# A four-layer graph network: a tile's gathered chunks are turned in four pieces between other steps, and the wait for a split load is rebuilt

## The chip, the cores and the metric

The kernel runs on one core of one Trainium2 chip. The metric is the device time of one execution, in microseconds (us). Engines are named as in the profile: PE (matmuls; PEld is its weight load), DVE (vector), ACT (scalar), POOL (GpSimd) and SP (which issues DMAs). One execution was also taken by the hardware profiler; all rows are of that execution.

## What is computed

Four graph layers run one behind the other on 3125 nodes of 128 features and 103125 edges sorted by destination, each as `x = x + layer(relu(layernorm(x)))`: a graph convolution, an attention with additive scores (4 heads), a second attention (GAT, 2 heads), and an interaction layer with a filter for each edge. The one that the change touches most is the additive attention:

```python
projected = (x @ W).reshape(N, HEADS, OUT_CH)          # 4 heads of 32
src = projected[row]
dst = projected[col]
scores = jnp.tanh(src + dst)
scores = jnp.einsum('ehc,hc->eh', scores, att)
scores = jnp.exp(scores - jnp.max(scores, axis=0, keepdims=True))
out = jax.ops.segment_sum(src * scores[:, :, None], col, num_segments=N)
normalizer = jax.ops.segment_sum(scores, col, num_segments=N)
out = out / jnp.maximum(normalizer, 1e-12)[:, :, None]
```

## The kernel before

The sorted edges are cut into 202 tiles of 512; a tile is four chunks of 128 edges, and its destinations lie in a window of 20 nodes. A stage (`Stage`) is one program for each engine, and semaphores alone order the engines against each other. `over_tiles` (L77) writes each engine's loop: it is given pairs of a lag and a piece of work, and in step s it calls each piece, in the order of the list, for tile s less its lag. So the list is the order of the engine's instructions, and a wait in one piece holds up all that is behind it. The steps of the first `head` rings are written out, the rest is a hardware loop.

`attend` (L1973) is that stage for both attention layers. The additive layer is the case `gat=False`: one bank of z per tile (`a.zs` is 1), 12 slots for gathered rows (`ring`), 6 for windows (`held`). In it

- SP loads, for two tiles at a time, the destinations and the window's rows (L1457, L1462); it waits for `z_ready` of a tile six earlier.
- POOL gathers the 512 source rows of a tile by four indirect DMAs of a chunk each (L897). Before a tile it waits for `sums_ready` of the tile that had its slot, 12 earlier.
- PE has four pieces. `scores` (lag 3) is one matmul with `far` (L2101) and one with `att` (L2109) and gives `score_ready`. `features` (lag 1) turns the four chunks by f32 transposes into the z bank (L2088), each once its chunk has landed, adds the window's rows by one matmul (L2092), and gives `z_ready`; ahead of that it waits for the window, for the one-hots, and for `act_ready` of the tile two earlier, which had the same z bank. `turn` (lag 4) transposes the raised scores (L2119, and in some steps the merge of running maxima, L1764 to L1777) and gives `turned`. `sums` (lag 5) is eight f32 matmul passes over the gathered rows (L2144) and gives `sums_ready`.
- ACT takes `exp` of the scores (L2178, lag 3), `tanh` of z (L2172, lag 1; it gives `act_ready`), and copies the sums (L2190, lag 5).
- DVE makes the one-hots (L1477, lag 0), finds the top score (L2228, L2230, lag 3), and copies the turned weights (L2246, lag 4), which gives `weight_ready`.

PE's order is set by the list in the last lines of its program: scores, features, turn, sums. In the GAT layer (`gat=True`) features has two heads, so eight transposes and two window matmuls, and its list is another.

`sum_counted` (L1348) is the second convolution's stage. It multiplies stored count matrices, in groups of 24 tiles (3000 KB a load), with node features. Before it, one tile's counts (`k.rebuild` is 1) are made again: DVE makes the one-hots, PE counts, ACT evicts, SP stores them (L1378) and waits for the store. The first group's 3000 KB are loaded in three thirds (L1375) ahead of that, each with a semaphore `begun[i]`; PE waits for `loaded[0]`, which SP gives after the store (L1387), and ahead of each third for `begun[i]` to reach a value held in a register, `k.rebuild * 16 + 16`. The next group's load is issued at L1390.

## Time and profile before

| what | value |
|---|---|
| time, median of 3 runs | 4942.16 us |
| lowest and highest run | 4939.04, 4942.38 us |
| the profiled execution's span | 4898.1 us, 89702 instructions |
| mean granted TensorE clock over the span | 0.852 |
| PE busy | 3999.0 us (82%) |
| POOL busy | 2828.1 us (58%) |
| DVE busy | 2847.4 us (58%) |
| ACT busy | 1737.4 us (35%) |

In the profile's rows "L2088" is line 2088 of the code, the arrow names the program's buffers, out<-in, and the brackets at a row's end hold the time for which the engine stood idle before it and what ended that. "issue" there is idle time in which the engine waited for nothing that the profile shows, and "remote" is an event that the profile puts down to no instruction. The additive loop fills 679 to 1922 us of the span and the GAT loop about 2100 to 3350.

### The profile page before, as it was taken

To read this page: it belongs to the slowest core of one execution; us is meant where nothing else is said; L and a number is where in the kernel's file an instruction comes from. 1 tells how busy PE (TensorE), PEld (TensorE's weight loads), DVE (VectorE), ACT (ScalarE), POOL (GpSimd) and SP (SyncE) were. 2 spreads that over 40 slices of the span, in tenths; PEclk is the share of its full clock that TensorE was granted. 3 is DMA by queue.
4 is the path that set the end of the run, shared out by engine and by line. 5 is a ranking of instruction groups with operands and counts; after the bars stand their busy time and mean duration, and the time that the engine had idled before them with its cause. 6 is when DMAs were issued, how large, how long until landed. Compare 5 with 4: busy or idle time off the path is not lost. (4 is left out here: it accounts for less than half of the span.)

```text
span 4898.1 us, 89702 instructions
## 1 busy us (share of the span) xinstructions
PE 3999.0 (82%) x22566; PEld 2260.3 (46%) x22566; DVE 2847.4 (58%) x8457; ACT 1737.4 (35%) x4474; POOL 2828.1 (58%) x3060
## 2 busy tenths in 40 slices
PE   3997927788887877488888888885399999999987
PEld 1344414445544544344444444442256655556652
DVE  7994032333333334555555555556678888888868
ACT  3773023344344334333333333331322222222227
POOL 0122356666666663555555555554368888888862
PEclk8998957776777777688988888886699999999999
DMA  2333422222222221333333333330056666666650
GB/s 80 91 87 103 147 71 57 57 56 57 57 56 57 56 57 27 113 98 96 97 97 96 96 97 96 97 96 18 21 97 104 105 105 104 104 105 104 104 110 13
DMA packets 377425, 402.41 MB, mean 82 GB/s; under 512 B 86457, under 2 KB 322502, under 8 KB 377030
## 3 DMA queue, kind: packets, MB, share of 16 engines
q0 software_dynamic: 151904, 198.72, 21.0%
q1 hardware_dynamic: 225382, 202.21, 14.4%
q8 instruction: 43, 0.70, 0.1%
q14 instruction: 96, 0.79, 0.1%
HBM read 312.91 MB, written 87.78 MB: 82 GB/s over the span
## 5 line engine op out<-in xcount | busy, mean ns | idle before, releaser
L897 POOL DMA_INDIRECT gathered<-table,sources x952 | 903.6, 949 | 600.6 <-issue 259.9
L1709 POOL DMA_INDIRECT sums<-gathered,idx x606 | 988.7, 1632 | 217.8 <-issue 166.4
L1571 PE MATMUL bank<-wide 128*128 128x512 bf16 x3636 | 851.5, 379 | 0.0
L2228 DVE TENSOR_REDUCE neg_raw<-bank 80x1 f32<-80x512 f32 (+1 forms) x404 | 276.6, 685 | 725.9 <-remote 252.1
L897 POOL DMA_INDIRECT wide<-table,sources x464 | 438.7, 946 | 275.1 <-issue 125.7
L1571 PEld LDWEIGHTS bank<-wide 128*128 128x128 bf16 x3636 | 347.7, 98 | 364.1 <-issue 1.7
L2178 ACT ACTIVATE msg<-bank,neg_top 80x512 f32<-80x512 f32 (+1 forms) x404 | 275.7, 682 | 643.1 <-DVE neg_top L2230 353.6
L1222 POOL TENSOR_TENSOR acc<-acc,msg 128x20 f32 x404 | 108.3, 268 | 411.2 <-issue 244.6
L2221 DVE TENSOR_TENSOR zact<-zact,bank 128x512 f32<-128x512 f32 x404 | 259.5, 683 | 123.1 <-ACT zact L2170 72.9
L2106 PE MATMUL bank<-zact,att_cells 128*32 128x512 f32 x808 | 289.4, 732 | 37.9 <-issue 36.2
L2088 PEld LDWEIGHTS bank<-ident,gathered 128*128 128x128 f32 x1360 | 191.8, 165 | 258.0 <-issue 232.2
L2109 PE MATMUL bank<-zact,att_cells 128*80 128x512 f32 x404 | 301.6, 838 | 6.6 <-issue 6.6
L2246 DVE COPY edge_rows<-bank 128x320 f32<-128x320 f32 (+1 forms) x404 | 183.2, 453 | 203.5 <-remote 132.7
L2144 PE MATMUL bank<-edge_rows,gathered 128*128 128x80 f32 x1088 | 193.9, 337 | 92.5 <-DVE edge_rows L2246 81.9
L2088 PE MATMUL bank<-ident,gathered 128*128 128x128 f32 x1360 | 237.4, 317 | 35.4 <-issue 26.4
L2119 PE MATMUL bank<-ident,msg 80*128 80x80 f32 (+1 forms) x1616 | 215.5, 262 | 61.5 <-issue 33.9
L897 POOL DMA_INDIRECT h_nm<-table,sources x200 | 189.4, 947 | 130.5 <-DMA wide<-table,sources 69.3
L2190 ACT COPY partial<-bank 32x20 f32 (+1 forms) x808 | 132.6, 164 | 357.5 <-remote 239.5
L1169 DVE TENSOR_SCALAR gathered<-iota_c,partial 128x500 f16<-128x500 f16 x808 | 257.6, 339 | 1.7 <-issue 1.3
L2170 ACT ACTIVATE zact<-bank 128x512 f32<-128x512 f32 x404 | 216.8, 588 | 98.1 <-DMA window<-parts 81.2
L1178 PE MATMUL bank<-gathered,zact 128*128 128x500 f16 x812 | 209.3, 381 | 49.4 <-ACT zact L1285 28.1
L1622 ACT COPY gathered<-bank 128x437 f32<-128x437 f32 x202 | 106.1, 525 | 337.0 <-PE bank L1597 249.7
(406 smaller groups left out, 7603.9 us busy)
## 6 DMA issues: line engine op xcount, KB each, us to landing
zact<-in_src_flat SPq DMA_DIRECT2D x202, 192.0 KB
edge_rows<-in_attr_rows SPq DMA_DIRECT2D x202, 128.0 KB
dst_pair<-local_rows SPq DMA_DIRECT2D x177, 128.0 KB
gathered<-table,sources POOLq DMA_INDIRECT x952
dst_pair<-local_rows SPq DMA_DIRECT2D x202, 64.0 KB
counts<-wide SPq DMA_DIRECT2D x4, 3000.0 KB
counts<-fm_ab SPq DMA_DIRECT2D x4, 3000.0 KB
fm_ab<-counts SPq DMA_DIRECT2D x4, 3000.0 KB, 11.0
```

The costliest lines, as they stand in the source:

```text
L897: pool.indirect_dma_start(out=g[:, j, :], out_offset=None, in_=table, in_offset=bass.IndirectOffsetOnAxis(ap=mine, axis=0)).then_inc(rows_ ...
L1169: hot = dve.tensor_scalar(k.cell_hot[slot][:, j, :], k.iota_c[:, :], own, None, ALU.is_equal)
L1571: pe.matmul(k.bank[b][:, :], k.split[t.two][:, c, :], k.source_hot[t.two][:, b * CHUNK:(b + 1) * CHUNK], start=first, stop=c == PARTS - 1, ...
L1709: pool.indirect_dma_start(out=k.sums[j], out_offset=bass.IndirectOffsetOnAxis(ap=k.idx[t.slot][:, j:j + 1], axis=0), in_=out_rows(t)[:, j, ...
L2088: pe.matmul(z_bank(t, h)[:, j * P:(j + 1) * P], g[:, j, h * F:(h + 1) * F], k.ident[:, :], is_transpose=True, start=(j == 0), stop=False, ...
L2106: mm = pe.matmul(score_bank(t)[own_cells(h), :], a.att[h][:, own_cells(h)], k.zact[t.two][:, h, :], start=False, stop=True, skip_group_che ...
L2109: mm = pe.matmul(score_bank(t), a.att[0][:, :], k.zact[t.two][:, 0, :], start=False, stop=True)
L2119: mm = pe.transpose(weight_bank(t)[:, j * cells:(j + 1) * cells], raised(t)[:, j * P:(j + 1) * P], k.ident[lanes(t), lanes(t)])
L2170: act.mul(k.zact[t.two][:, h, :], z_bank(t, h)[:, :], 0.2).then_inc(slope_ready, 1)
L2178: act.activation(raised(t), score_bank(t), ACT.Exp, bias=k.neg_top[lanes(t), bass.ds(t.t, 1)], accum_out=k.weight_sum[lanes(t), bass.ds(t. ...
L2221: m = dve.tensor_tensor(za, za, z_bank(t, h)[:, :], ALU.max)
L2228: dve.tensor_reduce(raw, score_bank(t), AX.X, ALU.max, negate=True).then_inc(top_found, 1)
```

## The change

In `attend`, `features` is cut into four functions: `features_begin` (the waits for the one-hots and the z bank, a semaphore increment, chunk 0), `features_second`, `features_third`, and `features_end` (the wait for the window, chunk 3, the window matmul, `z_ready`). In the additive layer PE's list becomes: first piece, scores, second piece, turn, third piece, sums, last piece. The GAT layer keeps one `features`, which calls the four in a row.

In `sum_counted` SP loads two thirds ahead of the store instead of three; after the store it waits for the second of them, tells PE by `second_there`, and loads the last third. PE waits for constants (or for the loop's counter) where it waited for a register's value.

```diff
--- before.py
+++ after.py
@@ -1354,6 +1354,7 @@
             hot_ready, counted, evicted, stored, free = (st.sem("hot_ready"), st.sem("counted"), st.sem("evicted"),
                                                          st.sem("stored"), st.sem("free"))
             loaded, begun = [st.sem(f"loaded{i}") for i in range(2)], [st.sem(f"begun{i}") for i in range(3)]
+            second_there, rounds_done = st.sem("second_there"), st.sem("rounds_done")
             summed, kept, adds_begun, added = st.sem("summed"), st.sem("kept"), st.sem("adds_begun"), st.sem("added")
             thirds = [(i * GROUP // 3, (i + 1) * GROUP // 3) for i in range(3)]
 
@@ -1367,18 +1368,26 @@
                 @block.sync
                 def _(sp):
                     sp.sem_inc(free, 1)
-                    for landed in begun:
+                    for landed in begun[0:2]:
                         sp.sem_inc(landed, 16)
+
+                    def load_third(i):
+                        lo, hi = thirds[i]
+                        sp.dma_start(k.counts[0][:, lo:hi, :], k.all_counts[lo:hi, :, :].rearrange(
+                            "t p c -> p t c")).then_inc(begun[i], 16)
                     with sp.Fori(0, k.rebuild) as n:
-                        for (lo, hi), landed in zip(thirds, begun):
-                            sp.wait_ge(landed, n * 16 + 16)
-                            sp.dma_start(k.counts[0][:, lo:hi, :], k.all_counts[lo:hi, :, :].rearrange(
-                                "t p c -> p t c")).then_inc(landed, 16)
+                        for i in range(2):
+                            sp.wait_ge(begun[i], n * 16 + 16)
+                            load_third(i)
                         sp.wait_ge(evicted, n + 1)
                         sp.dma_start(k.all_counts[bass.ds(tile(n), 1), :, :].rearrange("t p c -> (t p) c"),
                                      again).then_inc(stored, 16)
                         sp.wait_ge(stored, n * 16 + 16)
                         sp.sem_inc(free, 1)
+                        sp.wait_ge(begun[1], n * 16 + 32)
+                        sp.sem_inc(rounds_done, 1)
+                    sp.sem_inc(second_there, 1)
+                    load_third(2)
 
                     def load(now):
                         if now is None:
@@ -1409,6 +1418,7 @@
                     with pe.Fori(0, k.rebuild) as n:
                         pe.wait_ge(hot_ready, n + 1)
                         cell_counts(k, pe, 0, k.bank[0]).then_inc(counted, 1)
+                        pe.wait_ge(begun[0], n * 16 + 32)
 
                     def sums(now):
                         if now is None:
@@ -1416,8 +1426,10 @@
                         pe.wait_ge(loaded[now.par], (now.pair + 1) * 16)
                         wait_count(pe, kept, now.g - 1)
                         for i, (lo, hi) in enumerate(thirds if first(now) else [(0, now.size)]):
-                            if first(now):
-                                pe.wait_ge(begun[i], k.rebuild * 16 + 16)
+                            if first(now) and i == 1:
+                                pe.wait_ge(second_there, 1)
+                            if first(now) and i == 2:
+                                pe.wait_ge(begun[2], 16)
                             for b in range(k.blocks):
                                 mm = block_sums(k, pe, parts, now, b, lo, hi)
                         mm.then_inc(summed, 1)
@@ -2076,23 +2088,41 @@
             def _(pe):
                 turn_locals(k, pe, lo)
 
-                def features(t):
-
-                    pe.wait_ge(win_loaded[t.slot % held], (held_rounds(t) + 1) * 16)
+                def turn_rows(t, j):
+                    g = rows(t)
+                    pe.wait_ge(rows_loaded[t.slot][j], (t.rounds + 1) * 16)
+                    for h in range(a.zs):
+                        pe.matmul(z_bank(t, h)[:, j * P:(j + 1) * P], g[:, j, h * F:(h + 1) * F],
+                                  k.ident[:, :], is_transpose=True, start=(j == 0), stop=False,
+                                  skip_group_check=True)
+
+                def features_begin(t):
                     pe.wait_ge(onehot_t_ready, t.t + 1)
                     wait_count(pe, act_ready, t.t - 1)
-                    g = rows(t)
-                    for j in range(SUB):
-                        pe.wait_ge(rows_loaded[t.slot][j], (t.rounds + 1) * 16)
-                        for h in range(a.zs):
-                            pe.matmul(z_bank(t, h)[:, j * P:(j + 1) * P], g[:, j, h * F:(h + 1) * F],
-                                      k.ident[:, :], is_transpose=True, start=(j == 0), stop=False,
-                                      skip_group_check=True)
+                    pe.sem_inc(turns_begun, 1)
+                    turn_rows(t, 0)
+
+                def features_second(t):
+                    turn_rows(t, 1)
+
+                def features_third(t):
+                    turn_rows(t, 2)
+
+                def features_end(t):
+                    pe.wait_ge(win_loaded[t.slot % held], (held_rounds(t) + 1) * 16)
+                    turn_rows(t, 3)
                     for h in range(a.zs):
                         mm = pe.matmul(z_bank(t, h)[:, :], window(t)[0:WROWS, h * F:(h + 1) * F],
                                        place_hot(t)[0:WROWS, :], start=False, stop=True,
                                        skip_group_check=True)
                     mm.then_inc(z_ready, 1)
+
+                def features(t):
+
+                    features_begin(t)
+                    features_second(t)
+                    features_third(t)
+                    features_end(t)
 
                 def scores(t):
 
@@ -2155,7 +2185,8 @@
                     over_tiles(pe, k.tiles, [(3, scores), (1, features), (6, turn_sums), (4, turn_top), (4, turn),
                                              (5, sums)], ring=ring)
                 else:
-                    over_tiles(pe, k.tiles, [(3, scores), (1, features), (4, turn), (5, sums)], head=3, ring=ring)
+                    over_tiles(pe, k.tiles, [(1, features_begin), (3, scores), (1, features_second), (4, turn),
+                                             (1, features_third), (5, sums), (1, features_end)], head=3, ring=ring)
                     merge.tail_turns(pe)
 
             @block.scalar
```

## Rows read from the trace of the kernel before

**Rows 1.** The head of the page

```profile
span 4898.1 us, 89702 instructions
```

**Rows 2.** Windows view: stretch: its length, busy us by engine (count), PEclk, DMA

```profile
core 0: us, PE busy (x) PEld busy (x) DVE busy (x) ACT busy (x) POOL busy (x), PEclk, DMA share, GB/s
...
760.00:1890.00 1130.00, 922.40 (x3952) 559.86 (x3952) 374.47 (x1216) 456.90 (x1412) 704.04 (x744) 0.73 0.22 57
1893.00:1918.00 25.00, 23.68 (x146) 15.50 (x146) 14.66 (x52) 18.22 (x60) 0.00 (x0) 1.00 0.03 2
2120.00:3330.00 1210.00, 1024.93 (x7136) 537.89 (x7137) 684.53 (x1880) 383.77 (x939) 711.81 (x752) 0.88 0.33 96
```

**Rows 3.** Timeline, PE, end of the additive loop: start us, duration us

```profile
1896.12 0.41 PE L2101 MATMUL bank<-onehot_t,far 64*80 64x512 bf16 x1
...
1897.38 0.60 PE L2088 MATMUL bank<-ident,gathered 128*128 128x128 f32 x4
...
1898.23 0.50 PE L2119 MATMUL bank<-ident,msg 80*128 80x80 f32 x4
...
1899.55 0.41 PE L2101 MATMUL bank<-onehot_t,far 64*80 64x512 bf16 x1
```

**Rows 4.** Timeline, PE, one step at 1.2 GHz, same columns

```profile
1176.29 0.65 PE L2101 MATMUL bank<-onehot_t,far 64*80 64x512 bf16 x1
...
1182.62 0.65 PE L2101 MATMUL bank<-onehot_t,far 64*80 64x512 bf16 x1
```

**Rows 5.** Line L897 in 760:1890: what ended its engine's idle time, us, times

```profile
  issue: 208.5, 650
  remote: 163.5, 62
  PE bank L2144: 54.2, 32
```

**Rows 6.** Timeline, all engines, around 1115

```profile
1115.03 0.60 PE L2092 MATMUL bank<-onehot_t,window 60*128 60x512 bf16 x1
1115.42 0.94 POOL L897 DMA_INDIRECT gathered<-table,sources  x1 [0.30 <-issue]
...
1115.57 0.80 PE L2119 MATMUL bank<-ident,msg 80*128 80x80 f32 x4
1118.63 0.60 ACT L2172 ACTIVATE zact<-bank 128x512 f32<-128x512 f32 x1 [5.14 <-remote]
...
1118.92 0.47 DVE L2246 COPY edge_rows<-bank 128x320 f32<-128x320 f32 x1
...
1119.55 1.18 POOL L897 DMA_INDIRECT gathered<-table,sources  x1 [3.19 <-remote]
```

**Rows 7.** Timelines of DVE and POOL, opening stretch of the loop

```profile
732.82 0.49 DVE L2246 COPY edge_rows<-bank 128x320 f32<-128x320 f32 x1 [25.19 <-remote]
...
738.02 0.94 POOL L897 DMA_INDIRECT gathered<-table,sources  x1 [8.79 <-remote]
```

**Rows 8.** Waits view, PE, 760:1890: us, times, longest

```profile
PE bank L2144 <- DVE edge_rows L2246: 71.9, 25, 7.1
...
PE bank L2088 <- issue: 1.4, 3, 0.7
```

**Rows 9.** Sum_counted: timelines of SP and PE, then DMA issues (us to landing)

```profile
459.32 0.37 SPq L1378 DMA_DIRECT2D counts<-fm_ab  x1
...
465.17 0.45 PE L1195 MATMUL bank<-wide,h_nm 128*128 128x160 f16 x2 [6.74 <-SPq L1387]
...
482.63 0.57 PE L1195 MATMUL bank<-fm_ab,h_nm 128*128 128x480 f16 x2
...
wide<-counts SPq DMA_DIRECT2D x3, 1000.0 KB, 7.7
fm_ab<-counts SPq DMA_DIRECT2D x1, 3000.0 KB, 12.3
counts<-fm_ab SPq DMA_DIRECT2D x1, 125.0 KB, 5.5
```

## The prediction, made before the changed kernel ran

> **What bounds the kernel now.** I read the page's head first (span 4898.1 us, one core) [rows 1], then the windows view, stage by stage [rows 2]. The change touches three loops. In the additive loop (760 to 1890) 744 gathers, so 186 tiles of four, take 1130 us: 6.08 us a tile. PE is busy 922.40 us of it, at a mean granted clock of 0.73. Two rows at a granted clock of 1.00, one step apart, give PE's work for one tile alone: 1899.55 - 1896.12 = 3.43 us [rows 3]. At the lower level (1.2 GHz) the same step takes 1182.62 - 1176.29 = 6.33 us [rows 4]. So PE at the upper level would need far less than 6.08 and at the lower level more: the loop flips between the two, and PE's share says little.
>
> Next the gathers, by line: the groups of POOL's idle time before L897 [rows 5]. They add up to 208.5 + 163.5 + 54.2 = 426.2 us. A gather followed at once by the next shows 0.30 us, 744 x 0.30 = 223; the other 203 us are true waits, in 62 + 32 = 94 stretches: one per 1.98 tiles, 2.16 us long. Without them a tile costs POOL 4 x (0.94 + 0.30) = 4.97 us, the floor.
>
> What are these waits? The timeline around 1115 shows it [rows 6]. PE's window matmul is over at 1115.6, yet ACT's tanh, which needs it, starts at 1118.63 after idling 5.14 us; DVE's copy starts at 1118.92 though the turns it reads (L2119, seen at 1115.57) were over by 1116.4; POOL had begun its last gather at 1115.42. Three engines start within 0.3 us, and POOL 0.6 us later. In the opening stretch POOL streams 12 tiles of gathers: DVE idles 25.19 us before a copy, and POOL itself 8.79 us [rows 7]. So while gathers stream, what PE finishes reaches the others late, in bursts, and most reach them when POOL stops. I take as the bound: POOL's floor, plus a stop each time that PE has run dry of answers.
>
> The Trainium skill (page "SBUF — State Buffer", section "Who interferes with whom") says that DMA has its own ports and contends with no engine. By it these late starts would have some other cause than the gathers' traffic; the rows only show that they go together.
>
> **Additive loop: what is removed, added, moved.** The four turns of a tile's chunks (L2088) no longer stand together behind the scores, but one ahead of the scores, one behind them, one behind the turn, one behind the sums, and there the window matmul and z_ready. One sem_inc is added per tile. The engine work is the same: no matmul more or fewer. Were chunks late, pieces would help; PE's waits hold only 1.4 us (3 times) before L2088 in 186 tiles, against 71.9 us before L2144 [rows 8]. So the waits on chunks are worth nothing: 0 (bounds: -1.4 to +6, the latter 186 x 0.03 us for a sem_inc, a sixth of what POOL's smallest gap holds for waits and bookkeeping, an estimate).
>
> What changes is when z_ready comes: from behind the scores to the end of the step, 1899.55 - 1898.23 = 1.3 us later [rows 3], while its user stands where it stood or earlier: the first piece of tile t waits for the tanh of tile t-2 (same bank) and now heads the step, ahead of scores, turn and sums, which are queued behind it. Before, two whole steps lay between a tile's z and that wait; now one.
>
> The price by counting: a step gives four results, and I ask, from the moment when nothing more is passed on, how many PE can finish, the first withheld one included, until a wait needs an answer to a withheld one. A tile's turn comes one step behind its scores, its sums one step behind its turn.
> Order before (scores, features, turn, sums): scores first withheld: next step's turn stops PE, 6 done; features first: the turn after it is withheld too, next step's sums stop PE, 6; turn first: 5; sums first: 7. Mean 6.0.
> Order after (scores, turn, sums, features): scores first: 5; turn first: 5; sums first: 6 (stopped by the first piece two steps on); features first: 5, stopped by the same. Mean 5.25.
> A stretch now holds 1.98 tiles, eight results: six ahead and two that are passed on in between. With the same two, 7.25 instead of 8. Then 94 stretches become 94 x 8 / 7.25 = 103.7, each with 2.16 us: +21.0 us in 186 tiles, x 202 / 186 = **+22.8 us**. Bounds: 0, if bursts come by time and not by how far PE gets; +52, if PE's pace at 1.2 GHz becomes the pace (rival B). I take 22.8 because the wait that was longest before, L2144 on DVE's copy [rows 8], is of just this kind: turn to sums, a result and its answer.
>
> SP's window loads wait for z_ready of a tile six earlier, so they also go 1.3 us later, with some five steps in hand, 17 us at 3.43 and more at 6.08: 0. ACT and DVE keep their orders; the tanh is asked for beside the copy of the sums. 0.
>
> **GAT loop** (2120 to 3330) [rows 2]: the four pieces run back to back as before; the window wait stands behind three chunks instead of ahead, and a sem_inc per tile is added. POOL is busy 711.81 of 1210 us there, PE 1024.93, the clock 0.88. A window that is waited for later can only help, a sem_inc at 0.03 us costs 202 x 0.03 = 6 at most: 0, bounds -5 to +6.
>
> **sum_counted.** Three thirds of 1000 KB are in flight together (landing 7.7 us, median); the store of a tile's counts is issued at 459.32, lands after 5.5 us, and PE starts at 465.17 after 6.74 us [rows 9]. With two thirds ahead of it, the store has 1 MB less before it. The three thirds were 3.0 MB in 10.0 us by their median pace (7.7 us is the second of three, 3.85 us a third, less as the queue fills): the store gains at most one third, 3.5 us, less 0.4 for the issue of the last third that now stands ahead of the next load on SP, and the new wait on the second third lies before the store's landing. Taken: -2.6. The last third, then issued near 462.5, is needed at two thirds of the first group: PE needs 482.63 - 465.17 = 17.5 us for all, so 11.6 us later, and a third alone landed in under 7.7. The next group's load takes 12.3 us with 17.5 us of cover, 5.2 to spare; the last third ahead of it costs up to 3.5 of these. If that cover were gone, the rest would show as a wait ahead of the second group, +1. So **-2.6**, bounds -3.5 to +1.
>
> **Sum.** The profiled execution took 4898.1 us, the median of the runs 4942.2, so 44.1 us lie around the span and stay. 4898.1 + 22.8 - 2.6 = 4918.3; with 44.1: **4962.4**. Own range of this case: 4942 + 0 - 3 to 4942 + 45: 4940 to 4987.
>
> **Rivals.**
> A, the order doesn't matter. The bursts go by POOL's stops and not by how far PE gets; the four pieces give PE the same work in other order, and nothing waited for chunks [rows 8]. Left are -2.6 and the sem_incs: 4936 to 4946, 4940. For it: POOL resumes on the sums of a tile 12 back, far behind. Against it: the 71.9 us on one answer.
> B, slower still. The first piece, now at the head of a step, holds up all that is queued behind it until the tanh comes; PE stands idle more, its clock stays at 1.2 GHz, and PE's own step, 6.33 us [rows 4], takes the place of 6.08. 202 x (6.33 - 6.08) = +50.5, so 4990. It decides from where the tanh of a tile comes over one step behind its z; the idle 5.14 us before ACT's tanh [rows 6] is already longer than the 3.43 us step.
> C, faster. Between results PE now always has a piece of a turn to do: a stop for one answer is covered by pieces, its idle time (1130 - 922 = 208 us) is broken up, and the clock holds the upper level longer; or sums close earlier in a step, so that POOL's stretches run longer. Whole, POOL's floor: 202 x (6.08 - 4.97) = -224, 4718; a third of it: -75, so 4942 - 75 - 3 = 4864. For it: 2 of the 3 worst waits are for DVE and ACT, not for data. Against it: a piece takes 0.15 us (0.60 for four [rows 3]) and the waits are some 3 us long.
> The Trainium skill (page "TensorE: Matmul & The Clock Gate", section "HAM oscillation — how this bites in real kernels") says that idle gaps between bursts of matmuls send the clock to half and that keeping PE fed restores it. By that the pieces would bring case C; by the row (0.15 us) each is too short to fill a 3 us gap. The trace agrees so far that the clock is 0.73 here and 1.00 at the loop's end, where no gather runs [rows 2].
>
> **Chances.** Forecast 0.34, A 0.21, B 0.13, C 0.32. C is large because the loop stands 224 us over its floor and any change of phase between PE, ACT and POOL may win a part, where at most some 50 can be lost by B. Slower by over 0.2% (9.9 us, about what a measurement of this kernel can tell from no change): 0.34 + 0.13 = 0.47; within: 0.21; faster: 0.32. Range for 8 in 10: 4880 to 5015, which leaves out the larger part of C beyond its -62 (0.13) and what lies beyond B (0.06); the likeliest case's own range is 4940 to 4987.
>
> **What would show it.** Right: in the windows view the additive loop goes from 6.08 to some 6.19 us a tile, POOL busy the same; POOL's waits before L897 count over 100 instead of 94, of the same 2.2 us; PE has a new wait ahead of the first piece, on ACT's tanh, of some 10 us or more; L2144's wait is no larger. In sum_counted PE starts near 462.5 with no gap ahead of the last third. GAT within 5 us. B: clock near 0.5 and the first piece as PE's largest wait. C: clock over 0.8, or under 80 waits of POOL. A: the same counts with the work in other order. It would be wrong altogether if POOL's waits change in length and not in number, since the count alone carries my sum.

## The result

The changed kernel takes 4951.13 us, median of 19 runs, against 4942.38 us of 19 runs of the kernel before, timed beside it: a ratio of 1.0017, 95% interval 1.0011 to 1.0023, so 8.8 us slower. The direction is the forecast one. The size is not: the forecast was +20.2 us, and the measured loss lies below the 0.2% that the prediction drew as its own line.

The profile after, first the windows view of the two attention loops, columns as in [rows 2]:

```profile
760.00:1890.00 1130.00, 958.57 (x3868) 562.80 (x3868) 368.47 (x1194) 445.66 (x1382) 695.41 (x732) 0.69 0.21 56
2120.00:3330.00 1210.00, 1011.07 (x7015) 531.36 (x7015) 671.59 (x1846) 377.47 (x925) 699.01 (x739) 0.87 0.33 95
```

732 gathers, 183 tiles, in 1130 us are 6.17 us a tile (6.08 in [rows 2]; 6.19 was forecast). That near match is luck: `z_early_3`, below, whose order should have kept the old pace, has 732 gathers in the same window too. PE is busier, 958.57 for 922.40 us, at a mean granted clock of 0.69 for 0.73. What ended POOL's idle time before its gathers (us, times), to be set beside [rows 5]:

```profile
  issue: 197.7, 630
  remote: 186.3, 76
  PE bank L2174: 51.2, 26
```

76 + 26 = 102 stops of POOL, one per 1.79 tiles, where 103.7 in 186 tiles were forecast, also one per 1.79. (By this count `z_early_3` has 100.) They last (197.7 + 186.3 + 51.2 - 732 x 0.30) / 102 = 2.11 us. PE's waits in the same stretch (us, times, longest), the pieces of features at L2095, the sums at L2174:

```profile
PE bank L2095 <- issue: 49.1, 22, 6.1
PE bank L2174 <- DVE edge_rows L2277: 47.8, 21, 5.6
...
PE bank L2095 <- ACT zact L2203: 12.2, 4, 5.0
```

The new wait ahead of the first piece is there, 49.1 + 12.2 = 61.3 us; the long ones all stand behind the window matmul (L2115) that closes the step before. The wait for DVE's copy is down from 71.9 [rows 8] to 47.8.

In `sum_counted` the timelines of SP and PE and the DMA issues (us to landing) answer to [rows 9]:

```profile
459.78 0.37 SPq L1383 DMA_DIRECT2D counts<-fm_ab  x1
462.42 0.37 SPq L1376 DMA_DIRECT2D wide<-counts  x1
...
462.89 0.45 PE L1195 MATMUL bank<-wide,h_nm 128*128 128x160 f16 x2 [3.99 <-SPq L1396]
...
481.11 0.57 PE L1195 MATMUL bank<-fm_ab,h_nm 128*128 128x480 f16 x2
...
fm_ab<-counts SPq DMA_DIRECT2D x1, 3000.0 KB, 14.8
counts<-fm_ab SPq DMA_DIRECT2D x1, 125.0 KB, 2.2
```

The store lands after 2.2 us for 5.5, PE starts at 462.89 for 465.17, the last third costs no wait, and the second group follows at 481.11 for 482.63 without a gap.

These two profiles should not be subtracted, though. The span after is 4945.2 us, 47 more than before's 4898.1, when the medians differ by 8.8. The profiled execution of after took 4946.96 us, 1.8 more than its span. So what lies around a span is some 2 us, and the 44.1 us that the prediction put there were something else: the profiled execution of before was faster as a whole than its timed runs, of which the fastest took 4935.64 us. It looks like an execution on another chip. From its first gather to its last the GAT loop takes 1305.5 us there, and 1302.7 to 1310.3 us in the four traces of the chip on which before takes 4906 us (below); after's takes 1326.5 us, and the traces of two chips on which before takes 4942 and 4934 us have 1323.2 to 1330.8 us, all with the GAT loop as before. The additive loop differs in the same way, 1217.1 to 1222.6 us against 1235.4 to 1254.2, whatever its order. So the steps from [rows 2] and [rows 5] to the rows above show the chip more than the change.

### The profile page after: what moved, and what is told of

It reads as the page before. It is cut to its first block and busy times, and to the rows that moved or that the text cites. A ratio compares the mean times of both kernels' runs of the same rounds, so it can differ in the third digit from the quotient of the medians.

```text
span 4945.2 us, 89965 instructions
## 1 busy us (share of the span) xinstructions
PE 4063.0 (82%) x22463; PEld 2281.6 (46%) x22566; DVE 2847.9 (58%) x8457; ACT 1737.1 (35%) x4474; POOL 2830.2 (57%) x3060
## 5 line engine op out<-in xcount | busy, mean ns | idle before, releaser
L897 POOL DMA_INDIRECT gathered<-table,sources x952 | 904.2, 950 | 633.2 <-issue 258.8
L1583 PE MATMUL bank<-wide 128*128 128x512 bf16 x3533 | 829.2, 379 | 5.6 <-issue 0.2
L897 POOL DMA_INDIRECT wide<-table,sources x464 | 439.9, 948 | 277.4 <-issue 128.5
L2095 PE MATMUL bank<-ident,gathered 128*128 128x128 f32 x1360 | 331.3, 334 | 70.8 <-issue 48.6
L2095 PEld LDWEIGHTS bank<-ident,gathered 128*128 128x128 f32 x1360 | 213.1, 176 | 294.7 <-issue 293.7
L2139 PE MATMUL bank<-zact,att_cells 128*80 128x512 f32 x404 | 321.3, 889 | 0.0
L2203 ACT ACTIVATE zact<-bank 128x512 f32<-128x512 f32 x202 | 119.6, 592 | 478.6 <-remote 340.1
L897 POOL DMA_INDIRECT h_nm<-table,sources x200 | 189.3, 946 | 135.4 <-DMA wide<-table,sources 62.9
L2201 ACT ACTIVATE zact<-bank 128x512 f32<-128x512 f32 x404 | 216.8, 588 | 94.0 <-DMA window<-parts 76.8
L2149 PEld LDWEIGHTS bank<-ident,msg 80*128 80x128 f32 (+1 forms) x1616 | 174.3, 167 | 145.5 <-issue 132.8
L2174 PE MATMUL bank<-edge_rows,gathered 128*128 128x80 f32 x1088 | 182.3, 325 | 54.6 <-DVE edge_rows L2277 39.4
```

What stands on the lines that cost most here:

```text
L897: pool.indirect_dma_start(out=g[:, j, :], out_offset=None, in_=table, in_offset=bass.IndirectOffsetOnAxis(ap=mine, axis=0)).then_inc(rows_ ...
L1583: pe.matmul(k.bank[b][:, :], k.split[t.two][:, c, :], k.source_hot[t.two][:, b * CHUNK:(b + 1) * CHUNK], start=first, stop=c == PARTS - 1, ...
L2095: pe.matmul(z_bank(t, h)[:, j * P:(j + 1) * P], g[:, j, h * F:(h + 1) * F], k.ident[:, :], is_transpose=True, start=(j == 0), stop=False, ...
L2139: mm = pe.matmul(score_bank(t), a.att[0][:, :], k.zact[t.two][:, 0, :], start=False, stop=True)
L2149: mm = pe.transpose(weight_bank(t)[:, j * cells:(j + 1) * cells], raised(t)[:, j * P:(j + 1) * P], k.ident[lanes(t), lanes(t)])
L2201: act.mul(k.zact[t.two][:, h, :], z_bank(t, h)[:, :], 0.2).then_inc(slope_ready, 1)
```

## The experiments

The change's form of `sum_counted` (the mend) is in all of them, with its waits on constants, so `mend_alone` is the base. Each was timed beside the kernel before on the same chip: 11 runs (`far_twice` 6, `one_gather` 2 each time) against 17 to 33 of before. A "stop" is a stretch in which POOL waits between two gathers.

**The parts one at a time.** `mend_alone`: the change's `sum_counted`, both attention layers as before.

> Only sum_counted is changed (two thirds ahead of the store, constant waits); both attention layers are as before. Theory (look-ahead count): -2 to -3 us, PE starts the first group near 462.9 as in the changed kernel, and the additive loop runs at 6.08 us a tile with a stop of POOL per 1.98 tiles. Rival (the profiled execution of before, 4898.1, is not typical of its 4942): the additive and the GAT loop are longer here than in that profile, by up to 40 us together, and the time is still -2 to -3 us against before.

Measured: 4903.31 us, before 4906.45; ratio 1.0000 (0.9991 to 1.0009). The medians give -3.1 us, the means of the same runs +0.2, and the interval doesn't exclude 0. The chip was another: before takes 4906 us on it and 4942 on the first.

`order_alone`, on top of it the additive order; the GAT layer's `features` untouched:

```diff
-over_tiles(pe, k.tiles, [(3, scores), (1, features), (4, turn), (5, sums)], head=3, ring=ring)
+over_tiles(pe, k.tiles, [(1, features_begin), (3, scores), (1, features_second), (4, turn),
+                         (1, features_third), (5, sums), (1, features_end)], head=3, ring=ring)
```

> mend_alone plus the additive layer's order in four pieces; the GAT layer's features are untouched. Theory (look-ahead count): +20 us against mend_alone, POOL stops once per 1.79 tiles instead of 1.98. Rival (the order costs half of that, and before's profile was a lucky one): +8 to +13 us against mend_alone, and all that the changed kernel lost.

Measured: 4913.41 us, 1.0018 (1.0009 to 1.0027), +10.1 us against `mend_alone` by the medians and +7.9 by the means: the rival's size. The windows view and POOL's idle groups, `mend_alone` first, then `order_alone`:

```profile
760.00:1890.00 1130.00, 898.19 (x3912) 542.68 (x3912) 372.74 (x1210) 454.24 (x1401) 704.40 (x744) 0.74 0.22 57
...
  issue: 205.6, 658
  remote: 167.4, 61
  PE bank L2156: 52.9, 25
```

```profile
760.00:1890.00 1130.00, 952.22 (x3929) 560.45 (x3930) 374.57 (x1208) 454.57 (x1407) 709.16 (x744) 0.70 0.22 57
...
  issue: 203.4, 647
  remote: 155.3, 64
  PE bank L2185: 63.4, 33
```

The stops go from 61 + 25 = 86 to 64 + 33 = 97, 13% more, where 10% were forecast. But their sum goes from 425.9 - 223.2 = 202.7 to 422.1 - 223.2 = 198.9 us: each is shorter, 2.05 for 2.36 us. PE is busy 952.22 for 898.19 us at a clock of 0.70 for 0.74. PE's waits tell the same as in after's profile, here on one chip, `mend_alone` first:

```profile
PE bank L2156 <- DVE edge_rows L2258: 99.0, 32, 8.3
```

```profile
PE bank L2095 <- issue: 51.8, 30, 5.2
PE bank L2185 <- DVE edge_rows L2288: 45.1, 20, 5.1
...
PE bank L2095 <- ACT zact L2214: 15.7, 8, 5.1
```

But neither trace shows where the 8 to 10 us are. Both windows hold 744 gathers, and from the first to the last gather the loop takes 1222.2 us in `mend_alone` and 1222.5 in `order_alone`. The profiled execution of `mend_alone` was the slowest of its 11 runs (4913.48 us), that of `order_alone` the second fastest (4910.60 us), so one pair of traces can't resolve a difference of that size.

How the lengths of stops differ shows when POOL's timeline is sorted by how many tiles it gathered since its last stop (gaps of over 0.6 us between two gathers, without the first and last tiles; the length less the 0.30 us of every gap):

| kernel | 1 tile: stops, us | 2 tiles | 3 tiles |
|---|---|---|---|
| before | 10, 1.67 | 50, 2.10 | 20, 2.93 |
| after | 17, 1.67 | 61, 2.26 | 12, 3.04 |
| mend_alone | 3, 2.16 | 52, 2.17 | 23, 2.94 |
| order_alone | 19, 1.58 | 55, 2.02 | 14, 2.83 |

A stop behind one tile takes about 1.6 us (in the rows with ten or more), behind two 2.1, behind three 2.9. A line through these gives an estimate: some 0.65 us for each tile that is let through and 0.95 us for the stop itself. If the lengths come about in this way, only the second part is paid more often when the same tiles come in more stops. This was drawn up after the result, and the sums of the two traces don't confirm it: by it 11 more stops would add some 10 us, where the sum of `order_alone` is no larger.

`gat_alone`: the GAT layer's `features` in four calls in a row with the added increment, the additive layer as before.

> mend_alone plus the GAT layer's features in the new form (one more semaphore increment per tile, the window's wait behind three chunks); the additive layer is as before. Theory: within 3 us of mend_alone. Rival (the added increment is the GAT loop's +22 us of the two profiles): +10 to +22 us against mend_alone.

Measured: 4908.39 us, 1.0003 (0.9994 to 1.0012), +5.1 against `mend_alone` by medians (+1.1 by means) with intervals that overlap. The GAT stretch, `mend_alone` first, then `gat_alone`:

```profile
2120.00:3330.00 1210.00, 1027.50 (x7118) 538.62 (x7119) 684.17 (x1877) 382.96 (x938) 708.25 (x749) 0.87 0.34 96
```

```profile
2120.00:3330.00 1210.00, 1020.50 (x7137) 535.08 (x7136) 684.36 (x1873) 383.47 (x937) 711.60 (x750) 0.88 0.34 96
```

749 and 750 gathers in the same 1210 us: the same pace. The rival's 10 to 22 us fall; a loss up to 5 us stays possible. By medians the parts are -3.1, +10.1 and +5.1, together +12.1; by means they are +0.2, +7.9 and +1.1, together +9.2. The whole was measured at +8.8 by both.

**Place or pieces.** `whole_last`: features whole, at the step's end.

```diff
-over_tiles(pe, k.tiles, [(3, scores), (1, features), (4, turn), (5, sums)], head=3, ring=ring)
+over_tiles(pe, k.tiles, [(3, scores), (4, turn), (5, sums), (1, features)], head=3, ring=ring)
```

> mend_alone plus the additive order scores, turn, sums, features, with features whole: the window's result stands at the same place as in the change, with no pieces. Theory (look-ahead count; the place of a tile's result counts, not the pieces): as order_alone within 5 us. Rival (the pieces matter, as cover for a wait or by the first piece heading the step): more than 8 us from order_alone, on either side.

Measured: 4908.59 us, 1.0004 (0.9995 to 1.0013): +5.3 against `mend_alone`, 4.8 below `order_alone`, and 80 stops of over 0.6 us where `mend_alone` has 77 and `order_alone` 91. By the letter the time is within the 5 us of the theory, but the stops are not: the count of results ahead gives 5.25 here as for `order_alone`. Features waits for a tanh at the end of a step now, but the scores at its head wait for the same tanh, and there PE does wait in this trace (L2150, the matmul with `att`):

```profile
PE bank L2150 <- issue: 65.6, 12, 7.9
...
PE bank L2150 <- ACT zact L2213: 18.7, 8, 8.6
```

So two orders with one count have 80 and 91 stops. PE's clock fell all the same:

```profile
760.00:1890.00 1130.00, 916.63 (x3963) 547.25 (x3963) 373.98 (x1216) 458.13 (x1414) 712.24 (x748) 0.70 0.22 57
```

`z_early` is the counterpart, the first piece at the head and z where it was:

```diff
+over_tiles(pe, k.tiles, [(1, features_begin), (3, scores), (1, features_second),
+                         (1, features_third), (1, features_end), (4, turn), (5, sums)], head=3, ring=ring)
```

**The other way round.** `sums_later` puts the sums (PE) and their copy and merge (ACT) at lag 6; `all_later` puts the turn at 5 (and DVE's copy), sums, copy and merge at 7.

```diff
-over_tiles(pe, k.tiles, [(3, scores), (1, features), (4, turn), (5, sums)], head=3, ring=ring)
+over_tiles(pe, k.tiles, [(3, scores), (1, features), (4, turn), (6, sums)], head=3, ring=ring)
-                        (5, keep_sums), (5, merge_steps)], head=3, ring=ring)
+                        (6, keep_sums), (6, merge_steps)], head=3, ring=ring)
```

```diff
-over_tiles(pe, k.tiles, [(3, scores), (1, features), (4, turn), (5, sums)], head=3, ring=ring)
+over_tiles(pe, k.tiles, [(3, scores), (1, features), (5, turn), (7, sums)], head=3, ring=ring)
-                        (5, keep_sums), (5, merge_steps)], head=3, ring=ring)
+                        (7, keep_sums), (7, merge_steps)], head=3, ring=ring)
-over_tiles(dve, k.tiles, [(0, onehots), (3, tops), (4, edge_weights)], head=3, ring=ring)
+over_tiles(dve, k.tiles, [(0, onehots), (3, tops), (5, edge_weights)], head=3, ring=ring)
```

`one_gather` thins the stream: from the 13th tile on only the first chunk of each tile is gathered, so three quarters of the sources in the additive layer are left out, and PE waits for new rows of the first chunk alone (the code is shortened here):

```diff
-gather(k, pool, table, rows(t), gathers_begun, rows_loaded, t)
+if gat or n < ring:
+    gather(k, pool, table, rows(t), gathers_begun, rows_loaded, t)
+    continue
+pool.indirect_dma_start(out=rows(t)[:, 0, :], out_offset=None, in_=table, ...)
```

> mend_alone plus the additive order first piece, scores, second, third and last piece, turn, sums: the window's result stands where it stood before, the first piece still heads the step. Theory (count of results ahead): mean 6.0 as before, so within 4 us of mend_alone. Rival (the first piece's wait ahead of the scores, or pieces as such, cost the 10 us of order_alone): 7 to 13 us above mend_alone.

> mend_alone with the additive layer's sums (PE) and their copy and merge (ACT) one step later (lag 6): turn to sums is then two steps, the mean count 7.0 instead of 6.0. Theory, with the stop's length as the profiles of the first four runs show it (about 0.95 us and 0.65 us for each tile let through): 94 stops become 94 x 8 / 9 = 84, so -10 us against mend_alone. Rival (a stop costs its whole 2.16 us): -22 us. Second rival (the count means nothing): within 4 us, or slower since POOL has one slot less to run ahead.

> mend_alone with turn at lag 5 and sums, copy and merge at lag 7: every answer has two steps, mean count 7.75. Theory: 94 x 8 / 9.75 = 77 stops, -16 us against mend_alone at 0.95 us each. Rival (2.16 us each): -37 us. Second rival (no effect of the count): within 4 us.

> mend_alone, but from the 13th tile on POOL gathers one chunk of four in the additive layer (the other three keep the rows of the first tiles, so sources are left out). POOL's floor falls from 5.0 to 1.25 us a tile. Theory (what PE finishes is held up while gathers stream): answers come at once, the clock goes up, and the loop runs at 3.4 to 4.2 us a tile, -360 to -530 us. Rival (the late answers have another cause, the order's or the engines' own chain): the loop stays at 5 us a tile or more, -200 us or less.

Measured: 4380.63, 4378.61 and 4379.19 us, ratios 0.9991 (0.9982 to 1.0000), 0.9990 (0.9981 to 0.9999) and 0.9992 (0.9983 to 1.0001); `one_gather` 4108.34, -275.5: the expected pace, but from a loop that was at 5.0 us a tile already. The surprise is the kernel before: 4383.84 us on this chip. In `z_early`'s trace POOL hardly stops in the additive loop, and it runs at its floor, so no order can be told apart there. The four went again, with `order_alone` in the place of `one_gather`:

> The kernel of order_alone once more. On a chip where POOL stops as in the profiles of before (about 80 stops of over 0.6 us in the middle 172 tiles) theory: 1.001 to 1.003 of before, some 91 stops. On a chip like that of z_early, where POOL never stopped in the additive loop and before takes 4384 us, theory: the order costs nothing, 0.999 to 1.000 of before. Rival (the order costs PE something by itself): 1.002 on both.

> The kernel of z_early once more, for a chip on which POOL stops. Theory (count of results ahead, mean 6.0 as before): 0.9985 to 1.000 of before, the mend's -3 us included, stops as in mend_alone. Rival (a first piece that heads the step is what costs): 1.001 to 1.003.

> The kernel of sums_later once more, for a chip on which POOL stops. Theory (0.95 us for each stop saved): mean count 7.0, 0.996 to 0.9985 of before. Rival (2.16 us for each): 0.995. Second rival (the count means nothing): 0.999 to 1.001.

> The kernel of all_later once more, for a chip on which POOL stops. Theory (0.95 us for each stop saved): mean count 7.75, 77 stops for 94, 0.995 to 0.997 of before. Rival (2.16 us for each): 0.992. Second rival (the count means nothing): 0.999 to 1.001.

Again a chip of this kind (before 4379.91 us): 0.9993 (0.9984 to 1.0002), 0.9997, 0.9989 and 1.0001. So no cost of the order shows where POOL doesn't stop. The same kernel on the two kinds of chip, `order_alone` first, then `order_again`, in the opening stretch and in the loop:

```profile
680.00:730.00 50.00, 15.54 (x43) 6.74 (x42) 3.15 (x9) 2.74 (x6) 35.84 (x38) 0.53 0.22 58
760.00:1600.00 840.00, 718.10 (x2899) 422.17 (x2899) 276.62 (x888) 336.73 (x1043) 526.07 (x552) 0.68 0.22 57
...
  issue: 151.9, 478
  remote: 119.3, 51
  PE bank L2185: 44.5, 23
```

```profile
680.00:730.00 50.00, 40.77 (x155) 22.43 (x156) 15.82 (x36) 15.44 (x50) 37.79 (x41) 0.70 0.27 77
760.00:1600.00 840.00, 745.63 (x3575) 440.79 (x3574) 343.73 (x1111) 419.36 (x1275) 635.57 (x670) 0.86 0.24 69
...
  issue: 203.9, 669
  PE bank L2185: 0.3, 1
```

670 gathers in 840 us are 5.01 us a tile, the floor. While POOL streams the first twelve tiles, PE does 155 matmuls in the 50 us in which it did 43 on the other. ACT's tanh there and the window matmul of PE (L2115) that gives its input, `order_alone` first:

```profile
690.99 0.60 PE L2115 MATMUL bank<-zact,window 60*128 60x512 bf16 x1
...
697.87 0.60 ACT L2214 ACTIVATE zact<-bank 128x512 f32<-128x512 f32 x1 [8.15 <-remote]
...
725.06 0.60 PE L2115 MATMUL bank<-onehot_t,window 60*128 60x512 bf16 x1
...
730.77 0.60 ACT L2214 ACTIVATE zact<-bank 128x512 f32<-128x512 f32 x1 [20.71 <-remote]
```

```profile
688.62 0.60 ACT L2214 ACTIVATE zact<-bank 128x512 f32<-128x512 f32 x1 [1.07 <-PE bank L2115]
...
692.76 0.60 PE L2115 MATMUL bank<-onehot_t,window 60*128 60x512 bf16 x1
...
693.40 0.60 ACT L2214 ACTIVATE zact<-bank 128x512 f32<-128x512 f32 x1 [0.20 <-PE bank L2115]
```

In `order_alone` the window matmuls are over at 691.59 and 725.66, and the tanhs start at 697.87 and 730.77, 6.3 and 5.1 us later; the rest of the 20.71 us of idle time is PE's own delay, which waited for late answers itself. In `order_again` the matmul is over at 693.36 and the tanh starts at 693.40. A third try of the three came to a chip with stops (before 4942.34 us):

> z_early a third time, for a chip on which POOL stops (before at 4900 to 4950 us). Theory (count of results ahead, 6.0 as before): 0.9985 to 1.000 of before. Rival (a first piece that heads the step is what costs): 1.001 to 1.003. Where POOL never stops: 0.999 to 1.000 by both, and nothing is told apart.

> sums_later a third time, for a chip on which POOL stops. Theory (mean count 7.0, 0.95 us for each stop saved): 0.996 to 0.9985 of before. Rival (2.16 us each): 0.995. Second rival (the count means nothing): 0.999 to 1.001.

> all_later a third time, for a chip on which POOL stops. Theory (mean count 7.75, 0.95 us each): 0.995 to 0.997 of before. Rival (2.16 us each): 0.992. Second rival (the count means nothing): 0.999 to 1.001.

Measured: 4946.34, 4941.20 and 4945.25 us; 1.0003 (0.9994 to 1.0012), 0.9997 (0.9988 to 1.0006), 1.0000 (0.9991 to 1.0010). `z_early` lies between its theory and its rival, and its interval takes in both. `z_early_3` has 732 gathers in 1130 us, as many as after:

```profile
760.00:1890.00 1130.00, 896.40 (x3872) 529.93 (x3872) 366.95 (x1193) 447.06 (x1383) 694.08 (x732) 0.73 0.22 56
```

`sums_later` and `all_later` miss the theory: more results ahead bought nothing. They have 81 and 82 stops of over 0.6 us, `z_early` 82, as many as before's 83. Two rows of PE's waits show part of why, `sums_later_3` and `all_later_3`:

```profile
PE bank L2100 <- DVE onehot_t L1489: 45.6, 24, 5.3
```

```profile
PE bank L2156 <- issue: 85.3, 73, 2.7
PE bank L2100 <- DVE onehot_t L1489: 37.6, 18, 3.9
```

DVE makes a tile's one-hots behind its copy of older weights, in order, so a turn or a sum that is passed on late also keeps back the one-hots for the next features (L2100). My count had followed PE's own waits and not this queue. That these waits are what used up the gain is argued, not tested.

**What sets a stretch.** Two edits of `mend_alone`: `far_twice` gives PE more to do, `ring_eight` lets POOL be only 8 tiles ahead; `one_gather_2` is `one_gather` on a chip with stops.

```diff
+                    if not gat:
+                        pe.matmul(score_bank(t), a.far[:, :], place_hot(t)[0:HROWS, :], start=True, stop=True)
                     pe.matmul(score_bank(t), a.far[:, :], place_hot(t)[0:HROWS, :], start=True, stop=gat,
-                    wait_count(pool, sums_ready, n + 1 - ring)
+                    wait_count(pool, sums_ready, n + 1 - (ring if gat else 8))
```

> mend_alone with the first matmul of the additive layer's scores issued twice: PE has 0.34 us more a tile at the upper clock and 0.58 us at the lower, 69 to 117 us in 202 tiles, the results and their order the same. Theory (a stop of POOL and the answers set the pace, PE's own time lies inside): +0 to +15 us against mend_alone. Rival (PE's pace at a low clock is what a stretch of POOL covers, so the loss of the change is PE's longer work at a clock of 0.70 for 0.74): +40 us or more. Where POOL never stops: 0 to +5 by both.

> mend_alone, POOL held to 8 tiles ahead of the additive layer's sums instead of 12 (the wait's constant; the buffers stay). Theory (POOL stops when it has passed on the sums of the last stretch, so the depth doesn't matter): within 5 us of mend_alone and 2.0 to 2.2 tiles per stop. Rival (the stops come from a ring that is too shallow): 1.5 tiles per stop or fewer, +30 us or more. Where POOL never stops: near 0 by both.

> The kernel of one_gather once more (three of four chunks keep the rows of the first twelve tiles), for a chip on which POOL stops. Theory (what PE finishes is passed on late only while gathers stream): the additive layer runs near the 3.8 us a tile that it had on the other chip, where POOL never stopped, so -450 us against before. Rival (this chip passes PE's results on late whatever POOL does): 5 us a tile or more.

Before took 4933.96 us on this chip. `far_twice`: 4964.88 us, 1.0059 (1.0041 to 1.0076), +31 against before and some +34 against the base, between theory and rival. Its runs scatter more than the others' (4947.75 to 4976.87 us). Windows view and POOL's groups:

```profile
760.00:1890.00 1130.00, 971.87 (x4046) 559.07 (x4044) 365.26 (x1185) 441.03 (x1370) 688.80 (x728) 0.72 0.22 55
...
  remote: 175.1, 70
  PE bank L2158: 71.6, 37
```

70 + 37 = 107 stops in 182 tiles, and sorted as above 32 stops behind one tile, 53 behind two, 13 behind three (`mend_alone`: 3, 52, 23). PE's own time alone, with the count of results ahead as before, makes stretches shorter and stops more. The price of 0.95 us falls short here: 98 sorted stops for 78 are 20 x 202 / 172 x 0.95 = +22 us, and some +34 were measured. At 1.2 GHz two steps of PE are 2 x 6.33 = 12.66 us [rows 4], about what POOL needs for two tiles and a stop, 2 x 4.97 + 2.16 = 12.1.

`ring_eight`: 4925.97 us, 0.9981 (0.9972 to 0.9990), with 80 stops as before: the depth doesn't make the stops, as the theory said. Its time is at the edge of the theory's 5 us. That it gains 8 us, some 5 of them beyond the mend, was not expected, and no run here says why. It is the one kernel of this study with all its gathers that beats both the kernel before and the changed one on a chip with stops.

`one_gather_2`: 4464.35 us, -470 against before. The windows view of it and then of `one_gather`, from the chip without stops:

```profile
760.00:1400.00 640.00, 640.00 (x3768) 404.46 (x3768) 362.20 (x1165) 425.52 (x1342) 168.71 (x178) 1.00 0.16 41
```

```profile
760.00:1400.00 640.00, 640.00 (x3768) 404.51 (x3767) 362.67 (x1173) 432.31 (x1348) 166.31 (x176) 1.00 0.15 41
```

The two are alike: PE without a gap at a clock of 1.00, 178 and 176 gathers, one for a tile, so 3.6 us a tile with one gather each, near PE's own 3.43. On a chip where PE's results come late while four gathers a tile stream, they come in time when one does. So the stream of gathers goes with what holds them up, on chips of this kind and not on others: thinning it alone brought the answers in time. PE's turn and sums use the thinned rows like any others, so their time is the same.

The rule of the Trainium skill (page "SBUF — State Buffer", section "Who interferes with whom") that DMA has its own ports and contends with no engine fits the traces of the chips without stops (0.04 us from PE to ACT in `order_again`). On the others the late results need the gathers; which shared part it is, no run shows.

## Why the prediction was right or wrong

**What bounds the kernel.** Right: POOL's floor plus stops, stops from answers that come late while gathers stream. `one_gather_2`, `order_again` and `ring_eight` bear it out. The 25.19 and 5.14 us that the prediction quotes are idle times and not delays of one result; the delays that can be read are 3 to 6 us. That this holds on some chips alone couldn't be seen in one trace.

**The number of stops.** 10% more were forecast. `order_alone` has 13% more than its base (97 for 86), and only 7% more than the mean of three traces with the old order (94, 86 and 91 in before, `mend_alone` and `gat_alone`); of stops over 0.6 us it has 91 for 80. The new wait ahead of the first piece is there too. That after's profile gives one per 1.79 tiles, as forecast, is luck, since its chip gives 100 stops to `z_early_3` as well. And the count that gave the number is not the rule: it fits `order_alone` and `z_early_3`, but fails in `whole_last` (5.25 as well, and no more stops) and where it rose (`sums_later_3`, `all_later_3`); it left out DVE's queue, and `far_twice` moves the number without touching the count. A late z alone (`whole_last`, 1.0004) and a first piece at the head alone (`z_early_3`, 1.0003, on another chip) show no loss clear of noise; both together do (1.0018). Why is open. The one semaphore increment more per tile is no good candidate: `z_early_3` has it too.

**The price of a stop.** This is the step that failed: the prediction gave each of 9.7 more stops the mean length of 2.16 us, +22.8 us in all. In `order_alone` the stops were more and each was shorter, 2.05 for 2.36 us, their sum was 198.9 for 202.7 us, and the kernel lost 8 to 10 us. A likely reason is that the mean length holds the work of letting tiles through, which is paid once for each tile however they are bundled. The estimate of 0.95 us for one more stop gives 11 x 202 / 172 x 0.95 = +12.3 us (11 is 91 less the 80 of the old order, in 172 tiles), and with the forecast's own number 9.7 x 202 / 186 x 0.95 = +10.0. Both are near the +7.9 to +10.1 measured, but the estimate was made with these traces at hand, missed a third of `far_twice`, and no trace shows the lost time itself. At 2.16 us each, 11 x 202 / 172 = 13 more stops would have cost 28 us. So it is shown that 2.16 us is too much; what one more stop costs stays open. The prediction had named the danger: "wrong altogether if POOL's waits change in length and not in number"; both changed.

**PE's work.** "The engine work is the same" held for the instructions. But the clock fell from 0.74 to 0.70 and PE was busy 5.12 for 4.83 us a tile (952.22 / 186, 898.19 / 186). Case B had this as its mechanism and overrated it at +50: the 0.29 us a tile came out of PE's idle time, and the two windows hold the same 744 gathers. The lower clock is no consequence of more stops, nor does it make them by itself: `whole_last` has 0.70 with 80 stops, on the same chip, and `all_later_3` 0.71 with no more stops than `z_early_3`.

**sum_counted.** Right by the traces: -2.6 us forecast, PE 2.3 us earlier at the start, the last third without a wait. The times can't tell: -3.1 us by medians, +0.2 by means, with an interval that holds 0. (The "10.0 us" for three thirds stands in no row, and 3 x 3.85 is 11.6; the bound of 3.5 that was taken from it held, as the store landed 3.3 us sooner.)

**GAT.** Forecast 0, bounds -5 to +6; the pace of `gat_alone` is its base's, and +5.1 is within both bounds and noise. The 21 us by which this loop is longer in after's profile than in before's (1326.5 for 1305.5) go with the chip: `z_early_3`, whose GAT loop is as before, has 1330.8.

**The base.** "44.1 us lie around the span": wrong, some 2 us do. It shifted both sides alike, so the difference stood.

**The rivals.** A, the order doesn't matter: not refuted on the chips without stops, excluded on the others by `order_alone` (1.0009 to 1.0027). C, faster: no kernel with the additive order in pieces was, on a chip with stops.

## What to carry to other kernels

Where an engine stops again and again, its mean stop need not be the price of one more. Sorting the stops by how much work each lets through gives a first estimate of the part that doesn't grow with it, and the estimate wants a test of its own. Where a count is to predict the waits, test it with a second order that has the same count and should behave the same. Look for the queue behind the queue: a result that comes late also holds up whatever its reader would have done next. And before comparing two profiles, see whether a stage that the change doesn't touch has kept its length.

## What the runs showed of the hardware

Chips differ more than any edit here. The same kernel before took 4942, 4906, 4942 and 4934 us in four series and 4384 and 4380 us in two others, each within some 0.4% of itself. Each series of experiments ran on a chip of its own and none came back to one, so that it is the chip, and nothing else that changed between series, is inferred. On the second kind ACT's tanh starts 0.04 us after the matmul that it reads while POOL gathers without a pause (`order_again`, 693.36 and 693.40); on the first it starts 5.1 and 6.3 us after it in the same stretch (`order_alone`), and 3 us in the loop [rows 6], about when POOL stops. With one gather a tile both kinds give the same loop, 640 us of PE in 640 us at a clock of 1.00.
